# Second-layer query and output weights in one SBUF place, reloaded from DRAM twice a round

## What is computed

```python
# layer 0: adaptive layer norm, 16 heads of 32, keys and values through a latent of 128, block-sparse mask
h = (x - mu) * rsqrt(var + eps) * (1 + scale) + shift
q, c_kv = h @ Wq.T, h @ Wkd.T
k, v = c_kv @ Wku.T, c_kv @ Wvu.T            # 4 kv heads, rope on q and k
x = x + softmax(q k / sqrt(32), mask) v @ Wo.T
# layer 1: adaptive rms norm, 8 query heads of 64, one kv head, full attention, gated MLP
h = rms(x) * w1 * (1 + t @ tw1.T)
q, k, v = h @ Wq.T, h @ Wk.T, h @ Wv.T       # rope on q and k
x = x + softmax(q k / 8) v @ Wo.T
h = rms(x) * w2 * (1 + t @ tw2.T)
out = x + (silu(h @ Wg.T) * (h @ Wu.T)) @ Wd.T
```

## Time and profile before

| | us |
|---|---|
| median of 3 runs | 1803.69 |
| lowest and highest | 1802.77, 1805.55 |
| span of the profiled execution | 1804.9 |
| TensorE busy in it | 1717.2 |
| VectorE, ScalarE, GpSimd busy | 1152.3, 945.9, 398.8 |

### The profile page before, as it was taken

The page is one execution under the profiler, slowest core; times in us unless marked ns, Lnnn a source line. Parts: engine busy times, 40 slices in busy tenths (PEclk is TensorE's granted clock), DMA queues, the critical chain, the costliest instruction groups (busy, mean ns, idle before and its releaser), DMA issues.

```text
span 1804.9 us, 37773 instructions
## 1 busy us (share of the span) xinstructions
PE 1717.2 (95%) x12440; PEld 931.9 (52%) x12440; DVE 1152.3 (64%) x2858; ACT 945.9 (52%) x2769; POOL 398.8 (22%) x556
## 2 busy tenths in 40 slices
PE   6686899999999999999999999999999999999999
PEld 2344445555455545555455554555455554555444
DVE  6759566675667657685576756676576855767320
ACT  3836456364664538564483646645385644835320
POOL 3438587011111112111110111111121111101120
PEclk9676999999999999999999999999999999999999
DMA  7866489462784449662593637944485725936220
GB/s 245 152 181 115 126 197 253 98 117 82 163 175 94 80 119 184 133 118 78 127 194 91 119 88 161 171 95 82 115 192 125 123 73 138 196 85 112 100 70 24
DMA packets 527231, 234.30 MB, mean 130 GB/s; under 512 B 476336, under 2 KB 493744, under 8 KB 527024
## 3 DMA queue, kind: packets, MB, share of 16 engines
q1 hardware_dynamic: 511472, 175.09, 48.9%
q10 hardware_dynamic: 15552, 56.63, 10.1%
HBM read 90.09 MB, written 16.78 MB: 59 GB/s over the span
## 4 chain that ended last, share of the span: by engine, by line
PE 77%; DVE 10%; DMA 6%; issue 4%; ACT 2%; SPq 1%; DVEq 0%; POOL 0%; ACTq 0%
PE up L1427 8%; PE up L1429 8%; PE up L1428 8%; PE gate L1427 7%; PE gate L1429 7%; PE gate L1428 7%; PE y L1427 4%; PE y L1428 4%; PE y L1429 4%; PE bank L1427 4%; PE bank L1429 4%; PE bank L1428 4%; DMA prob_t<-prob 3%; PE bank L1454 2%; DVE prob L1113 2%
## 5 line engine op out<-in xcount | busy, mean ns | idle before, releaser
L864 ACT ACTIVATE bank<-bank,low 128x128 f32<-128x128 f32 (+2 forms) x768 | 302.7, 395 | 68.2 <-DVE low L1106 35.0
L702 POOL TENSOR_TENSOR inner_t<-inner,inner_t 128x512 f16<-128x512 f32 x128 | 149.0, 1164 | 662.7 <-ACT inner_t L1045 662.6
L1113 DVE TENSOR_TENSOR prob<-bank,prob 128x512 f16<-128x512 f32 (+1 forms) x320 | 202.8, 634 | 54.3 <-ACT prob L873 53.4
L873 ACT ACTIVATE prob<-bank 128x512 f16<-128x512 f32 (+1 forms) x320 | 178.7, 558 | 73.3 <-DMA prob_t<-prob 44.5
L1427 PE MATMUL up<-mlp,ring 128*128 128x512 f16 x512 | 194.9, 381 | 12.8 <-DVE inner L1392 12.8
L1382 DVE SCALAR_TENSOR_TENSOR silu<-silu,gate 128x512 f32<-128x512 f32 x128 | 87.9, 687 | 183.8 <-ACT silu L1039 183.0
L1427 PE MATMUL gate<-mlp,ring 128*128 128x512 f16 x512 | 194.0, 379 | 1.4 <-DVE mlp L1078 0.9
L1429 PE MATMUL up<-mlp,ring 128*128 128x512 f16 x512 | 194.9, 381 | 0.0
L1428 PE MATMUL up<-mlp,ring 128*128 128x512 f16 x512 | 194.9, 381 | 0.0
L1429 PE MATMUL gate<-mlp,ring 128*128 128x512 f16 x512 | 194.0, 379 | 0.0
L1428 PE MATMUL gate<-mlp,ring 128*128 128x512 f16 x512 | 193.9, 379 | 0.0
(11 more groups left out here) (182 smaller groups left out, 4041.8 us busy)
## 6 DMA issues: line engine op xcount, KB each, us to landing
ring<-wgu_dram ACTq DMA_DIRECT2D x108, 512.0 KB, 3.8
x_in<-x_dram SPq DMA_DIRECT2D x18, 512.0 KB, 3.8
x_res<-x_mid SPq DMA_DIRECT2D x16, 512.0 KB, 3.0
wgu_dram<-ring SPq DMA_DIRECT2D x16, 512.0 KB, 3.6
out_dram<-x_res SPq DMA_DIRECT2D x32, 256.0 KB, 2.3
prob_t<-prob SPq DMA_TRANSPOSE x256, 3.5
inner_t<-wd_t_dram SPq DMA_DIRECT2D x4, 1024.0 KB, 8.7
ring<-wg_t_dram SPq DMA_DIRECT2D x16, 256.0 KB, 4.1
```

The lines of the kernel that those rows point to most:

```text
L702: pool.tensor_tensor(inner_t[:, 1, f, :], inner[:], inner_t[:, 0, f, :], ALU.subtract).then_inc(inner_low, 1)
L864: ins = act.activation(bank_[:, at:at + wid], bank_[:, at:at + wid], ACT.Exp, bias=low[:, j % BANKS, k:k + 1], scale=-1.0, accum_out=total)
L873: act.activation(terms(prob[:, g % SLOTS, 0, :], layer, j), terms(work_bank[USE[f"unit{layer}", j] % BANKS][:], layer, j), ACT.Copy).then_ ...
L1113: dve.tensor_tensor(terms(prob[:, slot, 1, :], layer, j), terms(work_bank[USE[name] % BANKS][:], layer, j), terms(prob[:, slot, 0, :], lay ...
```

## The change

`wq1` and `wo1` get one place, `w1`, of the size of one of them. In round 0 GpSimd splits `wq1` into `w1` and `wo1` into `mlp`, which is unused until `fill4`. SP stores both to a DRAM tensor `w1s` at step `scores0` (`store_w1`), after waits on `big_split`. From then on `load_w1` brings in the output weights at `scores1` of each round (8 loads) and the query weights at `end` of each round but the last (7 loads), 1 MB each. TensorE waits on `w1_in` ahead of `query2` (from round 1 on) and of `finish` in layer 1.

```diff
-        wq1 = weight("wq1", CH, D)
-        wo1 = weight("wo1", CH, D)
+        w1 = sb("w1", [P, 2, CH, D], F16)
+        w1_halves = (w1[:, 0], w1[:, 1])
...
+        wo1_first = (mlp[:, 0], mlp[:, 1])
...
+            def load_w1(m):
+                sp.dma_start(w1[:].rearrange("p a c n -> p (a c n)"), w1s[m]).then_inc(w1_in, 16)
+
+            def store_w1():
+                for m, place in enumerate((w1, mlp)):
+                    sp.wait_ge(big_split, m + 1)
+                    sp.dma_start(w1s[m], place[:].rearrange("p a c n -> p (a c n)")).then_inc(
+                        w1_out, 16)
+
+            def swap_w1(n, step):
+                if step == "scores1":
+                    need_apart(sp, y_full, count(n, 8, 8), (cond_used, 1))
+                    load_w1(1)
+                elif step == "end":
+                    need_apart(sp, full, count(n, USES, USE["out1", PAIR - 1, TILES - 1] + 1),
+                               (cond_used, 1))
+                    load_w1(0)
...
                     store(m, step)
+                    if not last or step != "end":
+                        swap_w1(n, step)
...
+                if step == "scores0":
+                    store_w1()
+                elif step == "scores1":
+                    sp.wait_ge(w1_out, 32)
+                swap_w1((None, 0), step)
...
             def finish(n, m, layer, w):
+                if layer == 1:
+                    need(pe, w1_in, count(n, 32, 16))
...
+                if m is not None:
+                    need(pe, w1_in, count((n[0], n[1] - 1), 32, 32))
...
-                           "out1a.0": ["wo1"], "end": ["wd3"]}
+                           "end": ["wd3"]}
```

More of the change, by code:

```diff
@@ L233, in build @@
           ln2_w, tw2_t, wq1_t, wk1_t, wv1_t, wo1_t, wg_t, wu_t, wd_t, mask_c, rope0_c, freq_c,
-          wgu, out):
+          wgu, w1s, out):
     with ExitStack() as ctx:
@@ L371, in build @@
         ring_in = [sem(f"ring_in{m}") for m in range(RING)]
+        w1_in, w1_out = sem("w1_in"), sem("w1_out")
         gains_made, ident_zero, ident_made = sem("gains_made"), sem("ident_zero"), sem("ident_made")
@@ L452, in big_views @@
             slot = staged(key)
[L453 to L456, removed]
+            if key in ("wq1", "wo1"):
+                w = (w1_halves, wo1_first)[key == "wo1"][half]
+                return [(slot[:, c * D:(c + 1) * D], w[:, c, :]) for c in range(CH)]
+            at = int(key[-1]) * CH
+            return [(slot[:, c * D:(c + 1) * D],
+                     flat(wd[half])[:, (at + c) * D:(at + c + 1) * D]) for c in range(CH)]
         def raw_chunk(f):
@@ L1626, in layer1 @@
                     ins.then_inc(full, 1)
+                if m is not None:
+                    need(pe, w1_in, count((n[0], n[1] - 1), 32, 32))
                 for s in BOTH:
                     between(m, f"query2.{s}")
-                    queries(n, 1, s, 0, wq1)
+                    queries(n, 1, s, 0, w1_halves)
                 between(m, "keys1.0")
@@ L1633, in layer1 @@
                     between(m, f"query3.{s}")
-                    queries(n, 1, s, 1, wq1)
+                    queries(n, 1, s, 1, w1_halves)
                 for t in range(TILES):
@@ L1638, in layer1 @@
                 units(n, m, 1)
-                finish(n, m, 1, wo1)
+                finish(n, m, 1, w1_halves)
                 for s in BOTH:
@@ L1801 @@
     args["wgu"] = nc.dram_tensor("wgu_dram", (FCH, P, 4 * D), F16, kind="Internal").ap()
+    args["w1s"] = nc.dram_tensor("w1s_dram", (2, P, 2 * CH * D), F16, kind="Internal").ap()
     args["out"] = nc.dram_tensor("out_dram", (SEQS, TOK, D), F32, kind="ExternalOutput").ap()
```

## The result

| | before | after |
|---|---|---|
| median, us | 1803.37 | 1831.53 |
| lowest and highest | 1802.77, 1805.55 | 1830.21, 1832.89 |
| span of the profiled execution | 1804.9 | 1829.8 |

The ratio is 1.0152, with a 95% interval from 1.0138 to 1.0167: the changed kernel is slower by 27.4 us (24.9 to 30.1). The forecast was 25 us slower, at 1829.

The account below looks back on a forecast made before the run. TensorE, busy 95% of the span, was taken as the bound. Round 0's stores 12.4, eight loads at `scores1` 12.8, loads at `end` 0 and TensorE's waits 0 sum to 25.2 us; 1803.7 + 25.2 = 1829 us, range 1813 to 1843.

Parts of the forecast that it names:

- The bound: TensorE, busy 95% of the span; a loop of score copy, subtraction and transpose runs just ahead of it.
- Stores in round 0: At `scores0`, SP's wait for the split and the store delay the first `prob` transpose; 12.4 us lost.
- I take none back: In round 0, none of the 12.4 us delay is won back, as ScalarE sets the pace and cannot work ahead.
- The rival that the clock would win 24 us: TensorE gets full clock in three round 0 stretches, 24.0 us less, loads absorbed: 1792 us; chance 0.03.
- Loads at scores1: Each of eight loads delays the first `prob` transposes behind it, stalling TensorE 1.6 us: 12.8 us in all.
- the chain of the prediction: At `scores1`, late transpose landing delays unit 3's copy, unit 4's subtraction, then unit 8's scores: 1.6 us stall.
- the term of 12.8: Eight loads at `scores1`, each stalling TensorE 1.6 us in layer 1's attention units: 12.8 us.
- the first term: Cost of round 0's wait and stores at `scores0`: 12.4 us.
- the second: Cost of the eight loads at `scores1`: 12.8 us.
- The rival of absorbed loads: Transposes catch up in the DMA engines' 15% idle time; only round 0 pays, 1816 us; chance 0.2.
- What would show it: Profile signs: round 0 transpose at 66, 1.6 us gap per round, loads landing in 4.5 to 5.5 us.
- Loads at end and TensorE's waits: Seven loads at `end` hidden by 18 us of room, and two new TensorE waits a round: zero cost each.

Follow-up runs that it names:

- e6: Changed kernel with a second, unused 1 MB load ahead of each real load at `scores1`; 1854.14 us, ratio 1.028 to the kernel before.
- e5: Kernel before with only SP's wait for the second split added at `scores0`, no stores or loads; 1811.32 us, ratio 1.0042.
- e8: Changed kernel with stores behind round 0's layer 0 units and output weights loaded in four 256 KB pieces among the units on SP's queue; 1809.42 us.
- e2: Changed kernel with the eight output-weight loads issued by ScalarE on its own queue, ahead of its first layer 1 exponents; 1822.51 us, ratio 1.0107.
- e11: Changed kernel with stores behind round 0's layer 0 units and each output-weight load moved earlier on SP's queue, to `stack2.1`; 1803.53 us, ratio 1.0.
- e3: Changed kernel without the eight loads at `scores1`, so layer 1's output product uses the query weights; 1816.96 us, ratio 1.0076.
- e9: Changed kernel with stores behind round 0's layer 0 units and without the eight loads at `scores1`; 1805.18 us, ratio 1.0012.
- e7: Changed kernel loading only the high half of the output weights at `scores1`, 512 KB in place of 1 MB; 1814.87 us, ratio 1.0063.
- e1: Changed kernel with the two stores moved behind the 24 units of layer 0 in round 0; 1819.69 us, ratio 1.0091 to the kernel before.
- e10: Changed kernel with stores behind round 0's layer 0 units and output weights in four 256 KB pieces issued by ScalarE on its own queue; 1821.85 us.
- e4: Changed kernel without the seven loads at `end` and without TensorE's wait ahead of `query2`; 1830.99 us, ratio 1.0152 to the kernel before.
- e12: Changed kernel with stores behind round 0's layer 0 units and each output-weight load on SP's queue at `stack3.0`; 1817.65 us, ratio 1.008.

## Why the prediction was right

**The bound** was read rightly: TensorE kept its work, and the time grew by what it waits for.

**Stores in round 0**, 12.4 predicted, 12.15 at ScalarE's fourth copy. The steps held one by one: the issue came at 67.4 (66.1 predicted; GpSimd's last subtraction was itself 1.7 late in this execution), the landing took 5.2, less than the 5.9 that the forecast took for transfer and landing together. "I take none back" was too strict: on the way to layer 1 the shift falls from 12.15 to 9.6, and what the term cost is 9.6, or 2.8 less than forecast. Some 1.7 of this is TensorE's clock. In the output products at the end of layer 0, the granted clock (second column from the end is the DMA share, the one before it the clock) was, before and then after:

```profile
98.00:104.00 6.00, 6.00 (x29) 2.47 (x28) 1.85 (x3) 0.94 (x3) 0.00 (x0) 0.57 0.74 168
104.00:110.00 6.00, 3.96 (x43) 2.40 (x42) 3.29 (x7) 2.33 (x6) 0.00 (x0) 1.00 1.02 383
110.00:116.00 6.00, 6.00 (x22) 2.39 (x21) 1.18 (x2) 0.72 (x2) 0.19 (x1) 0.72 1.00 325
```

```profile
110.00:116.00 6.00, 6.00 (x37) 2.55 (x34) 1.85 (x3) 1.58 (x4) 0.00 (x0) 0.76 0.72 143
116.00:122.00 6.00, 4.38 (x40) 2.58 (x39) 3.68 (x7) 1.92 (x4) 0.00 (x0) 0.81 1.04 389
122.00:128.00 6.00, 5.35 (x22) 2.12 (x20) 1.40 (x4) 0.72 (x2) 0.89 (x2) 0.90 1.08 367
```

The output products fell into stretches at 0.57 and 0.72 before and at 0.76 and 0.90 after; TensorE lies 12.3 behind at the start of the first and 10.6 at the end of the last. The rival that the clock would win 24 us had its sign right here and its size wrong by more than ten times.

**Loads at scores1**, 1.6 each predicted, 1.5 in rounds 1 to 7, and the chain of the prediction (landing, copy of unit 3, subtraction of unit 4, scores of unit 8) is the one in the trace. The transfer of 2.9 us was right: 6.0 against 3.1 to landing. In e6 the transpose is issued 0.35 later and lands 2.1 later still, and the second megabyte costs 2.9. In round 0 the units of layer 1 lose 1.3, from the first copy to the last. So the term of 12.8 came to 11.9.

**What the forecast had no term for** follows just after these units of round 0. There 2.5 us more are lost, and the granted clock rises to full later, seen from the last copy (176.95 before, 188.77 after). Before, then after:

```profile
176.00:178.00 2.00, 2.00 (x31) 1.23 (x28) 1.26 (x3) 1.55 (x6) 2.00 (x3) 1.00 0.90 174
```

```profile
188.00:190.00 2.00, 2.00 (x36) 1.78 (x34) 1.26 (x3) 1.37 (x4) 2.00 (x3) 0.50 0.98 189
190.00:192.00 2.00, 2.00 (x7) 0.79 (x6) 0.21 (x1) 0.00 (x0) 1.68 (x5) 0.65 0.67 131
```

At 0.50, 1.2 GHz, the products with the values and the first output products take about twice as long: multiplications of 128x512 start every 0.43 us instead of 0.21. The other traces show how this loss goes with the clock in the 2 us behind the last copy. "Units" is what the units of layer 1 lost from the first copy to the last, "after them" what was lost from there to the start of round 1:

```
                     before  e5    e8    e2    e11   e3    e9    e7    e1    e10   after
units, us            0       0.0   -0.1  -0.1  -0.1  -0.1  0.0   0.1   1.9   1.5   1.3
clock behind them    1.00    1.00  1.00  1.00  1.00  0.84  0.85  0.84  0.50  0.50  0.50
after them, us       0       0.0   0.1   0.4   0.4   1.2   1.1   1.2   2.5   2.5   2.5
```

The remaining three, e4, e6 and e12, lost 1.8, 4.2 and 1.4 in the units; there the clock is full behind the last copy, falls to 0.50 again 10 us later, and 2.5 to 2.7 are lost. So units that run late come with a loss of 2.5 behind them whatever the lateness, and punctual ones with 0 to 1.2. The load brings between 1.3 and 2.5 of it, by the moment at which TensorE's work meets the clock. All of this was read from the traces; no run changed the clock alone.

The near hit is therefore partly luck: the first term was 2.8 too high and the second 0.9, the clock took 2.5 for which there was no term, and the trace after began 0.9 late.

**The rival of absorbed loads** named the idle 15% of the DMA engines as its reason. Loads are absorbed up to 512 KB (e7), and the whole megabyte is when it stands elsewhere (e11); what takes them up at `scores1` is the loop's margin ahead of TensorE, some 1.4 us (2.9 late, 1.5 paid), and not the mean share of idle engines. **What would show it** held but for one sign: the loads land in 6.0 (5.2 to 6.4), not 4.5 to 5.5. **Loads at end and TensorE's waits** at zero: e4 and e9 bear it out.

The rule of the Trainium skill (DMA: Bandwidth & Descriptors, "Queues, rings and completion order") that each engine takes descriptors in ring order agrees with the traces: behind 512 KB, 1 MB and 2 MB (e7, the changed kernel, e6) the transpose lands after 4.7, 6.0 and 8.1 us instead of 3.1, while the query transpose issued just ahead of the load, at 1011.25, lands in 3.1. By the same page's 6.15 us for 1 MB on GpSimd's path ("Bandwidth") the loads would have cost 38 us, an estimate; here a megabyte holds the queue 2.9.

## What to carry to other kernels

A DMA is priced by what stands behind it in its queue and by when that is needed, not by its bytes: the same two stores and 15 loads cost 27 us, 16 (e1) or nothing (e11), by their place. Before adding one to a queue that feeds the busiest engine's loop, find the first transfer behind it whose result is needed at once, and put the new one ahead of that by more than its own length (2.9 us here). Here one query transpose in between was not enough (e12, 2.0 us ahead), and two of them with an output store were (e11, 6.7 us ahead). A wait in a queue that is written out by hand holds all that stands behind it, so a store that nobody needs soon goes behind the work that somebody does.

## What the runs showed of the hardware

SP can be held while it issues a transpose behind a load. The first `prob` transpose of the units takes it 1.23 us to issue before. Behind one megabyte it took 1.23 in the changed kernel and 3.88 in e12, behind two 2.81 in e6. What sets this was not looked for.

SP goes on later at the end of a loop round. Before, 3.2 us lie between the last output store and the residual copy. After it is 7.2, and in e4, which has no load there, still 6.1, though its last store lands in 2.5 us:

```profile
1067.41 0.33 SPq L591 DMA_DIRECT2D out_dram<-x_res  x1
1073.55 1.16 SPq L585 DMA_DIRECT2D x_res<-x_mid  x2
```

It appears in the rounds of the hardware loop only and in every kernel whose SP program is longer in the loop, along with some 20 more packets of an instruction queue (q14, 99 before, 119 to 121 in these, 99 in e5). It may be the fetching of code at the jump back, which no run tested. It costs nothing here: in the changed kernel the copy starts at 1075.1, and what it reads is overwritten from 1090.1 on.
